# One attention program with its setup inside, batch 0 split on two engines, the top-token search spread over two turns, and the weights turned one group a unit

## What is computed

```python
x = x + _layernorm(_L0_attn_ref(_layernorm(x), ...))
x = x + _layernorm(_L0_ffn_ref(_layernorm(x), ...))   # top_k(scores, 128) per batch
x = x + _layernorm(_L1_attn_ref(_layernorm(x), ...))  # top_k(m, 35) per head
x = x + _layernorm(_L1_ffn_ref(_layernorm(x), ...))
```

## Time and profile before

| what | us |
|---|---|
| median of 3 runs | 2881.6 (2872.1 to 2886.0) |
| the profiled execution | 2883.1 |
| its span, first to last instruction | 2881.3 |
| busy in it: PE | 2537.3 (88%) |
| busy in it: DVE | 1708.3 (59%) |
| busy in it: ACT | 1199.1 (42%) |
| busy in it: POOL | 914.3 (32%) |

### The profile page before, as it was taken

The page is one execution under the profiler, slowest core; times in us unless marked ns, Lnnn a source line. Parts: engine busy times, 40 slices in busy tenths (PEclk is TensorE's granted clock), DMA queues, the critical chain, the costliest instruction groups (busy, mean ns, idle before and its releaser), DMA issues. The chain is left out here.

```text
span 2881.3 us, 40813 instructions
## 1 busy us (share of the span) xinstructions
PE 2537.3 (88%) x14324; PEld 1509.3 (52%) x14324; DVE 1708.3 (59%) x4753; ACT 1199.1 (42%) x1949; POOL 914.3 (32%) x1444
## 2 busy tenths in 40 slices
PE   3699999999999999999628999966999899999997
PEld 2244445454444445443316888844566665666664
DVE  2667676775867677678748754725444254344442
ACT  1166665666666665656313332122232222222321
POOL 6040352606143251704041211113323315224142
PEclk9699999999999999999658999978999999999999
DMA  2434061524326051531110211231112111011010
GB/s 93 132 100 109 24 193 54 182 54 147 105 72 180 24 177 53 172 98 48 45 57 9 71 53 65 82 103 60 31 37 67 30 45 60 31 59 45 16 44 30
DMA packets 156167, 220.28 MB, mean 76 GB/s; under 512 B 18639, under 2 KB 123035, under 8 KB 149724
## 3 DMA queue, kind: packets, MB, share of 16 engines
q1 hardware_dynamic: 151868, 213.65, 24.3%
q0 software_dynamic: 4096, 4.01, 0.5%
HBM read 113.75 MB, written 103.88 MB: 76 GB/s over the span
## 5 line engine op out<-in xcount | busy, mean ns | idle before, releaser
L1064 ACT ACTIVATE pt<-ps 128x1024 f32<-128x1024 f32 (+3 forms) x768 | 601.7, 812 | 306.5 <-PE ps L962 210.8
L856 DVE CUSTOM_DVE_ANT_0 masked<-ps,mask_q 128x128 bf16<-128x128 f32 (+3 forms) x1024 | 473.3, 485 | 244.9 <-PE ps L940 242.4
L940 PE MATMUL ps<-sk,sq 96*128 96x512 bf16 (+3 forms) x1536 | 427.8, 337 | 65.3 <-DMA sk<-scratch_stacks 27.5
L959 PE MATMUL ps<-sq,sk 99*128 99x512 bf16 (+3 forms) x1536 | 399.9, 329 | 13.7 <-DMA sq<-scratch_nm_parts 11.7
L860 DVE TENSOR_REDUCE mx<-ps 128x1 f32<-128x512 f32 x512 | 351.8, 687 | 90.7 <-PE ps L940 90.3
L940 PEld LDWEIGHTS ps<-sk,sq 96*128 96x128 bf16 x1536 | 132.3, 97 | 384.1 <-issue 101.3
L978 PE MATMUL ps<-pt,val 128*32 128x512 f32 (+3 forms) x3072 | 327.7, 499 | 3.3 <-ACT yt L1072 3.3
L2267 PE MATMUL ps<-w_fc,eyb 128*128 128x256 f32 x1024 | 229.7, 382 | 13.7 <-ACT eyb L2328 7.8
L959 PEld LDWEIGHTS ps<-sq,sk 99*128 99x128 bf16 x1536 | 148.2, 98 | 156.5 <-ACT pt L1064 52.5
L2255 PE MATMUL ps<-eht,w_fc 128*128 128x512 f32 x512 | 224.3, 596 | 1.5 <-ACT eht L2318 1.5
L2267 PEld LDWEIGHTS ps<-w_fc,eyb 128*128 128x128 f32 x1024 | 192.9, 191 | 47.5 <-ACT eyb L2328 16.1
(11 more groups left out here) (335 smaller groups left out, 4370.9 us busy)
## 6 DMA issues: line engine op xcount, KB each, us to landing
scratch_stacks<-space SPq DMA_DIRECT2D x32, 768.0 KB, 4.0
sq<-scratch_stacks SPq DMA_DIRECT2D x32, 768.0 KB, 8.7
sk<-scratch_stacks SPq DMA_DIRECT2D x32, 768.0 KB, 9.9
scratch_stacks<-space SPq DMA_DIRECT2D x32, 512.0 KB, 5.0
scratch_x<-xr SPq DMA_DIRECT2D x16, 1024.0 KB, 7.6
space<-in_L_attn_x SPq DMA_DIRECT2D x8, 1024.0 KB, 14.0
scratch_stacks<-space SPq DMA_DIRECT2D x32, 256.0 KB, 5.5
xr<-in_L_attn_x SPq DMA_DIRECT2D x8, 1024.0 KB, 6.3
```

The source lines that it names most:

```text
L856: nc.vector.tensor_tensor_reduce(mem["masked"][:, slot, 0:n], ps[:, RING[slot], 0:n], mem["mask_q"][:, BANK - n:BANK], 1.0, -3e38, ALU.add ...
L940: nc.tensor.matmul(ps[:, bank, 0:n], sq[0:ROWS, h, i * P:(i + 1) * P], sk[0:ROWS, h, half * BANK:half * BANK + n], start=True, stop=True)\
L959: last = nc.tensor.matmul(ps[:, bank, 0:n], sk[0:ROWS_M, h, j * P:(j + 1) * P], sq[0:ROWS_M, h, q0:q0 + n], start=True, stop=not diag)
L1064: nc.scalar.activation(pt[:, u % 3, 2 * pair:2 * pair + 2, 0:n], ps[:, bank:bank + 2, 0:n], ACT.Exp, scale=SCALE).then_inc(e["exp_done"], 1)
```

## The change

It has these parts:

- The setup is no program any more. `attention_setup` returns five functions that issue its parts inside the attention program: x of batch 0 is now SP's first load; POOL's and DVE's first instructions stand at the head of their streams; the rotation of the weights stands on DVE between x_stat and x_norm of batch 0; PE's bias products stand behind the four "xt" of batch 0. Its small tables lie in the buffer att. The memset of ones over sk comes on POOL behind batch 0's parts. The barrier and the clearing between setup and attention go; waits on `made`, `biased`, `prepared`, `masked` and `ones_in` come in their place.
- Of batch 0's eight halves of parts DVE does six and POOL the first half of k in each chunk. Stack 0 is loaded behind chunk 0, stacks 1 and 2 behind chunk 1.
- `EARLY_B` is 5, `LATE_B` 3. The scores of the first five batches are turned in unit 1 of turn 6; the 16 rounds stand in every fifth unit from unit 6 of turn 6 (the last is unit 33 of turn 7), "tok" in unit 42 of turn 7.
- The weights are staged in two steps, the first with `L1_attn_Wo` in a buffer of its own ("spare"). Their 20 groups are turned one a unit: 11 in units 20 to 30, 9 in units 33 to 41 of turn 7.
- In the attention's tail "t2" of tile i stands before "proj" of tile i - 1.
- The second program has new tables of places. By them five ranking rounds instead of two precede the first k_t on DVE, the last round and "tok" come half a batch earlier, "pick" of batch 5 is the first to wait for them, "up" comes behind "o" and "val" behind "s" on PE, and SP has load b, store_q b, load b + 1, ... where it had load b + 1 before store_q b.

The diff, cut to its core:

```diff
-EARLY_B = 6
+EARLY_B = 5
...
+    def begin_sync(sp):
+        sp.dma_start(mem["x"][:, :, :], io["x"][0].rearrange("(j p) c -> p j c", p=P)).then_inc(e["x_in"], 16)
+        with nc.allow_non_contiguous_dma(reason="a few columns of a bias"):
+            for dst, src in loads:
+                sp.dma_start(dst, src).then_inc(loaded, 16)
+
...
+    def setup_vector(v):
+        v.wait_ge(loaded, 16 * len(loads))
...
+        nc.vector.tensor_copy(w["ident16"][:, :], w["ident"][:, :])
+        nc.vector.drain()
+        nc.vector.memset(groupf[:, :], 0.0).then_inc(turned, 1)
+        v.wait_ge(cols, 1)
+        nc.vector.tensor_copy(w["bqk"][:, :], ps[:, 6, 0:2 * KC]).then_inc(biased, 1)
+        v.wait_ge(rows, 1)
+        nc.vector.tensor_tensor(w["bias_proj"][:, :], ps[:, 5, 0:C], bproj[:, :], ALU.add).then_inc(prepared, 1)
...
+        nc.vector.drain()
+        v.wait_ge(masked, 1)
...
+    def setup_tensor(pe):
+        pe.wait_ge(turned, 1)
+        for n in range(2 * KC):
+            last = nc.tensor.matmul(ps[:, 6, n:n + 1], brot[0:1, n * P:(n + 1) * P], one[:, :],
+                                    start=True, stop=True)
+        last.then_inc(cols, 1)
+        for k in range(KC):
+            last = nc.tensor.matmul(ps[:, 5, 0:C], bvrep[:, k, :], w["wproj"][:, k, :],
+                                    start=(k == 0), stop=(k == KC - 1))
+        last.then_inc(rows, 1)
...
 STAGED = (
-    (("sq", (("L0_ffn_W_qkv", 0), ("L0_ffn_W_out", 1536))), ("sk", (("L0_ffn_W1", 0), ("L1_attn_Wq", 1536)))),
+    (("sq", (("L0_ffn_W_qkv", 0), ("L0_ffn_W_out", 1536))), ("sk", (("L0_ffn_W1", 0), ("L1_attn_Wq", 1536))),
+     ("spare", (("L1_attn_Wo", 0),))),
     (("sq", (("L0_ffn_W2", 0), ("L1_attn_Wk", 1536))), ("sk", (("L0_ffn_W3", 0), ("L1_attn_Wv", 1536)))),
-    (("sq", (("L1_attn_Wo", 0),)),),
 )
...
+def parts_on_vector(step):
+
+
+    _, b, r, chunk, n = step
+    return b == 0 and (r, n) != (1, 0)
...
-            put(behind + 10 + i, ("proj", b, i))
+            if i:
+                put(behind + 9 + i, ("proj", b, i - 1))
+        put(behind + 17, ("proj", b, NT - 1))
...
-        put(now + 37 + n // 2, ("weights", B - 1, n))
-    put(now + 29, ("scores", B - 1, 0))
+        put(now + (20 + n if n < 11 else 22 + n), ("weights", B - 1, n))
+    put(now - turn + 1, ("scores", B - 1, 0))
     for n in range(ROUNDS_C):
-        put(now + 34 + n, ("top", B - 1, n))
-    put(now + 52, ("tok", B - 1))
+        put(now - turn + 6 + 5 * n, ("top", B - 1, n))
+    put(now + 42, ("tok", B - 1))
...
-    order += [("xt", 0, n, k) for n in range(NHALF) for k in range(KC)]
+    order += [("xt", 0, n, k) for n in range(NHALF) for k in range(KC)] + [("setup", 0)]
     for chunk in range(KC):
         for r in range(2):
             order += [("qk", 0, r, chunk, n) for n in range(NHALF)] + [("parts", 0, r, chunk, n) for n in range(NHALF)]
-    order += [("stack", 0, s) for s in range(SETS - 1)] + [("v", 0, 0, n) for n in range(NHALF)]
+        order += [("stack", 0, s) for s in ((0,), (1, 2))[chunk]]
+    order += [("v", 0, 0, n) for n in range(NHALF)]
     order += [("max", 0, 0, n) for n in range(len(MU))] + [("nmax", 0, 0), ("rows", 0, 0), ("nm", 0, 0)]
...
-        setup_attention(nc, io, w, ps, mem)
...
+                elif kind == "stack" and step == ("stack", 0, SETS - 2):
+                    g.wait_ge(e["parts_ready"][1], NHALF * KC)
+                    nc.gpsimd.memset(mem["sk"][ROWS:P, :, :], 1.0).then_inc(e["ones_in"], 1)
+                elif kind == "parts" and not parts_on_vector(step):
                     r, chunk, n = a
                     half = slice(n * BANK, (n + 1) * BANK)
                     until_taken(g, ("qk", b, r, chunk, n))
-                    done = nth[step]
+                    done = pool_parts[step]
...
+                if step == ("x_norm", 0, 0):
+                    setup_vector(v)
+                elif kind == "parts" and parts_on_vector(step):
+                    r, chunk, n = a
+                    half = slice(n * BANK, (n + 1) * BANK)
+                    until_taken(v, ("qk", b, r, chunk, n))
+                    if chunk:
+                        v.wait_ge(e["parts_out"][r], 16 * len(RUNS[r]))
+                    nc.vector.tensor_copy(part[:, r, 0, half], qk[:, r, half])
+                    nc.vector.drain()
+                    nc.vector.tensor_tensor(qk[:, r, half], qk[:, r, half], part[:, r, 0, half], ALU.subtract)
+                    nc.vector.drain()
+                    nc.vector.tensor_copy(part[:, r, 1, half], qk[:, r, half])
+                    nc.vector.drain()
+                    nc.vector.tensor_tensor(part[:, r, 2, half], qk[:, r, half], part[:, r, 1, half], ALU.subtract)\
+                        .then_inc(e["parts_ready"][r], 1)
                 if kind == "top":
...
+                        if b == 0 and s == 0:
+                            pe.wait_ge(e["prepared"], 1)
+                            pe.wait_ge(e["masked"], 1)
...
+                        if b == 0 and s == 0:
+                            pe.wait_ge(e["ones_in"], 1)
...
-                    if halves_before(b, *a) >= NHALF:
+                    if halves_before(b, *a) == 0:
+                        act.wait_ge(e["biased"], 1)
+                    elif NHALF <= halves_before(b, *a) < (KC + 1) * NHALF:
+                        act.wait_ge(e["parts_ready"][r], halves_before(b, r, chunk, 0))
+                    elif halves_before(b, *a) >= NHALF:
...
-    0, 151.5, 157.5, 165.5, 169, 173.5, 180, 185.5, 192, 192.5, 205, 210.5, 224.5, 230, 233, 233.5,
+    0, 96, 96.5, 105, 108, 114, 119.5, 124.5, 133.5, 139, 150.5, 151, 165, 167, 179.5, 188.5,
 )
-TOK_AT = (239, 240)
+TOK_AT = (191, 188.5)
 
```

More of the change, by code:

```diff
@@ L360, in weight_groups @@
         for buffer, names in places:
-            place = mem[buffer][:, s * HS:(s + 1) * HS, :].rearrange("p h t -> p (h t)").bitcast(F32)
+            if buffer == "spare":
+                place = mem["spare"]
+            else:
+                place = mem[buffer][:, s * HS:(s + 1) * HS, :].rearrange("p h t -> p (h t)").bitcast(F32)
             for name, at in names:
@@ L599, in attention_loop @@
             .rearrange("p (r a t) -> p r a t", r=2, a=PARTS)
-        names = """padded gains_in sc_out sc_in idx_ready
+        names = """loaded made masked zeroed turned cols rows numbered biased prepared ones_in padded gains_in sc_out sc_in idx_ready
             x_in x_stat head_step x_rstd x_ready
@@ L670, in until_split @@
                 engine.wait_ge(e["parts_out"][2 * chunk + r], 16 * len(RUNS[r]) * B)
+    begin_sync, begin_gpsimd, begin_vector, setup_vector, setup_tensor = attention_setup(nc, io, w, ps, mem, e)
+    pool_parts, halves = {}, 0
+    for step in order:
+        if step[0] == "parts":
+            pool_parts[step] = halves
+            halves += not parts_on_vector(step)
     with nc.Block() as block:
@@ L674, in _ @@
         def _(sp):
+            begin_sync(sp)
             for step in order:
@@ L751, in _ @@
         def _(g):
+            begin_gpsimd(g)
             for step in order:
@@ L826, in _ @@
         def _(v):
+            begin_vector(v)
             for step in order:
@@ L916, in _ @@
                         pe.wait_ge(taken[slot], uses)
-                if kind == "weights":
+                if kind == "setup":
+                    setup_tensor(pe)
+                elif kind == "weights":
                     s, turns, _ = groups[a[0]]
@@ L983, in _ @@
                     n, k = a
+                    if b == 0:
+                        pe.wait_ge(e["made"], 5)
                     pe.wait_ge(e["x_ready"], NT * b + 4 * (n + 1))
@@ L1138 @@
 PRODUCTS_AT = {
-    ("hnt",): (148, 143), ("q_t",): (152, 153), ("k_t",): (157.5, 153.5), ("s", 0): (159, 159.5),
[7 rows of a table removed]
+    ("hnt",): (105.5, 103.5), ("q_t",): (110, 111), ("k_t",): (112, 113), ("s", 0): (114.5, 115),
[7 rows of a table added]
 }
 OTHERS_AT = {
-    ("l1",): 133, ("xs",): 139, ("hn",): 141.5, ("pick",): 149, ("r1",): 157.5, ("less", 0): 160.5,
-    ("exp", 0): 161.5, ("exp", 1): 163, ("less", 1): 163, ("hn2",): 188, ("r2",): 205, ("load",): 207,
-    ("x2",): 208.5, ("xn2",): 211, ("r3",): 223, ("r4",): 225.5, ("put",): 230, ("samp",): 240.5,
-    ("store_q",): 240.5,
+    ("l1",): 93, ("xs",): 96, ("hn",): 98, ("pick",): 107.5, ("r1",): 111, ("exp", 0): 115.5, ("exp", 1): 117,
+    ("less", 0): 117, ("less", 1): 118, ("hn2",): 144.5, ("r2",): 155, ("x2",): 165, ("xn2",): 168.5, ("r3",): 177,
+    ("r4",): 181.5, ("put",): 189, ("samp",): 191.5, ("load",): 207.5, ("store_q",): 210.5,
 }
 RANKS_AT = (
-    0, 151.5, 157.5, 165.5, 169, 173.5, 180, 185.5, 192, 192.5, 205, 210.5, 224.5, 230, 233, 233.5,
+    0, 96, 96.5, 105, 108, 114, 119.5, 124.5, 133.5, 139, 150.5, 151, 165, 167, 179.5, 188.5,
 )
-TOK_AT = (239, 240)
+TOK_AT = (191, 188.5)
 def mod_order():
```

241 lines of the change are left out of this document (99 added, 142 removed), and 14 rows, old and new, of the table PRODUCTS_AT.

## The result

| | before | after |
|---|---|---|
| median of the runs | 2880.4 us (17 runs) | 2889.4 us (17 runs, 2885.4 to 2894.9) |
| ratio to before | | 1.0039, 95% interval 1.0028 to 1.0050 |
| span of the profiled execution | 2881.3 us | 2890.6 us |
| mean granted clock | 0.945 | 0.949 |

The changed kernel is 9 us slower, by my bound of 0.5% no change. I had forecast 2854, with 2822 to 2880: the time lies outside. The gains that I counted came, the two large ones larger than I said. Three costs took them back, of which I had one at six tenths of its size, one at a sixth and one at nothing.

A forecast was written before the change was run, and what follows sets the result against it. PE was taken to set the pace of the attention (busy 156.1 of 163.8 us in turn 6), with 48 us of slack on DVE. Sum: 2883.1 - 30 + 35 - 33 - 3 + 2 = 2854 us, range 2822 to 2880.

The forecast's parts named there:

- start: Start of the attention: first products at 59 to 60 instead of 89.1, -30 us (bounds -24 and -34).
- steady turns, swap of t2 and proj: Steady attention turns: the swap costs nothing, since exp products stand between the two steps either way.
- top rounds in turns 6 and 7: Turns 6 and 7: each of 16 DVE rounds stalls PE 2.2 us, +35 in all (bounds 0 and 64).
- weights: Weight groups moved from the last unit set into units 20 to 35: -3 us (0 to -7).
- tail: Attention's tail: 21 to 22 us at full clock where 55.0 stood, -33; -24 if the clock falls anyway.
- POOL chain: 38.7 us of POOL work after the attention's projections, expected to stay unchanged.
- second program: Second program ranks three batches instead of two, five rounds ahead of the first k_t: +2 us (bounds -2.5 and +9.5).
- rival (c): Stalls let the clock fall: rounds cost 64 + 22 = 86, total 2905; sign, turn 6 clock under 0.95. Chance 0.05.
- Rival (b): Each round stalls PE its full 4.0 us, 64 in all: 2883, no change; sign, turn 6 30 longer. Chance 0.17.
- Rival (d): Second program's late start not made up, new order worse: +12, 2866; sign, over 8 us longer. Chance 0.08.
- rival (a): Turns 6 and 7: rounds absorbed to about 0.5 us each, 2827; sign, turn 6 unchanged. Chance 0.15.
- The price that the prediction drew from it: Start: by the shared-port lock POOL's 3.7 us would be added to the chunk, making the start worth -26.

The follow-up runs named there:

- e5: Changed kernel with the sixteen top rounds back behind the last nmax, one a unit from unit 34 of turn 7, still five early batches: 2859.8 us, ratio 0.9934.
- c1: Changed kernel with six early batches, old second-program lists, old t2/proj order in batches 0 to 6, rounds only where DVE serves nobody: 2810.9 us, ratio 0.9766.
- the control: Another name for e5, the changed kernel with the sixteen top rounds back behind the last nmax: 2859.8 us, ratio 0.9934.
- e2: Changed kernel with the old order (proj of a tile ahead of t2 of the next) for batches 0 to 6: 2874.5 us, ratio 1.0008.
- e3: Changed kernel with the second program's sixteen rounds placed later, one instead of five ahead of the first k_t: 2899.3 us, ratio 1.0093.
- e7: Changed kernel with the second program's old slot lists, its rounds over slots 0 and 151.5 to 217, tokens at 220: 2886.3 us, ratio 1.0028.
- e4: Changed kernel with all halves of q and k of batch 0 split on POOL, as before the change: 2897.8 us, ratio 1.0084.

## Why the prediction was wrong

By its own steps, predicted and found:

| step | predicted | found |
|---|---|---|
| start | -30 | -32.2 at the first nmax |
| steady turns, swap of t2 and proj | 0 | +12.0 up to batch 6 |
| the same swap in turns 6 and 7 | 0 | +1.4 and +1.6 |
| top rounds in turns 6 and 7 | +35 | +59.7 |
| weights | -3 | +2.5 in turn 7, -5.8 in the last set |
| tail | -33 | -38.5 |
| POOL chain | 0 | +0.1 |
| second program | +2 | +12.4 |
| third program | 0 | -3.8 |
| sum | -29 | +9.3 (9.4 by the rounded rows) |

The rows of turns 6 and 7 come from kernels that differ there in one part: the rounds from the changed kernel less e5; the swap from e5 less before in turn 6 and from e5 less c1 in turn 7; the weights in turn 7 from c1 less before (c1 has them at their new units, but neither the swap nor a round ahead of the last nmax). Single profiles scatter by some tenths of a us there, so rows of 1 to 3 us are rough.

**The start** went as described: q,k products at 29.59 (30.0), the first cast of a half at 34.05 (34.5), sk asked for at 49.98 (50), first product at 56.85 (59 to 60). A half took DVE 2.5 us alone, as worked out from the slopes. Two sizes were off and partly cancel: beside POOL the splitting of chunk 0 ended at 43.5 instead of 42.0, and the load of sk took 6.9 us instead of 10.0.

**The rounds** are the largest miss, 25 us, and the failing step is "a stall of 2.2 us a round, 16 x 2.2 = 35", taken as the whole price. PE's idle is 35.6 us in sixteen rounds, my 35. I had the other half of the price in hand, in rival (c): that stalls let the clock fall, at 2.7 us for half the rounds, 1.35 a round. It came at 24.1, or 1.5 a round. I had it decide only in a world in which each round stalls PE by 4.0, and argued from turn 6 before the change, where waits of under 1 us leave 1.00. The 2.4 us waits are another kind. The idle part and the clock part belong in one sum; that sum, 35 + 22, would have given 2876. Rival (b) had 64 for the rounds, close to the 59.7, but by a stall of the full 4.0 each; its total would be near by luck. Of the signs I set, three came: turn 6 over 30 us longer (b), a granted clock under 0.95 there (c), the second program over 8 us longer (d). The Trainium skill, page "TensorE: Matmul & The Clock Gate", section "A second HAM failure mode: psum-queue depth-cycling", describes a clock that swings when short idles cut groups of products while the banks cycle. The trace agrees: 1.00 in the control's turn 6, 0.92 with nine rounds in it, and half rate in the products right behind a round.

**"In the steady turns the swap costs nothing: exp products stand between the two steps either way"** is the second failing step. By e2 it costs 1.9 us in each of turns 1 to 5, some 9 of the 12.0, and by the ledger 3 more in turns 6 and 7. The rest of the 12.0 is mostly one set of batch 2, 45.1 us instead of 41.7, which is 43 to 46 in all kernels with the new start: there the returned maxima are late once, 2.3 us of PE wait, and the set's clock is 0.96. Why they are late there I have not followed.

**The second program** failed at "But those 12 us are then missing from the stretch to 1625". The first kbd came 9.8 later, as worked out (9.5), but what the later stretch gave back was not kept: kbd of batch 4 was 4.8 behind before, that of batch 6 9.0, and the end 12.4. Rival (d) had +12 on the sum with a chance of 0.08; found is +10.4 on it. Its reason was not right: neither the late start (e3) nor the new order (e7) makes the loss, but the third late batch.

**The tail** ran at full clock; a tile cost PE 1.09 us instead of the 1.5 I took, and it is 16.5 where I had 21 to 22. I put the full clock down to the missing rounds; by e5 the projections have it in the new order even with the rounds back, so in the last batch the swap is worth some 14 us by itself, about what it costs in the turns before. **The weights** came out net -3.3 for -3: 2.5 paid in turn 7, 5.8 back in the last set.

The chances: 0.73 on faster leant on rival (a), absorbed rounds, for a fifth of it. Nothing was absorbed. Three terms erred the same way, rounds, swap and second program by 50 us together, and the start, the tail and the third program gave only 11.5 back; the range of 26 us upwards did not hold two misses at once.

## What to carry to other kernels

Price a long instruction on the consumer of a short ring twice: by its length less what the ring covers, and by the clock of the producer after the stall, here 2.2 + 1.5 us for a block of 4.0. Cutting it helped by half only; the place for it is where nobody waits for its engine, and such places can be found in the trace as windows in which another engine's serial chain runs: six of sixteen rounds fitted into a POOL chain for nothing. A change with several parts is worth taking apart: the start and the last batch's order of this one, with its rounds moved and without its steady order and its third late batch, took 2811 us where the kernel before took 2881.5 on the same chip.

## What was not expected of the hardware

DVE and POOL make each other wait while both split halves in SBUF. Beside POOL a cast of 512 columns on DVE took 1.05 and 1.22 us instead of 0.43, a subtraction 0.94 instead of 0.69; beside DVE, POOL's first cast took 0.89 instead of 0.61 and its subtraction 1.48 instead of 1.15. A half cost POOL 4.8 instead of 3.7 and DVE 4.1 instead of 2.5. The two streams of the changed kernel, merged in order of time:

```profile
38.66 1.48 POOL L780 TENSOR_TENSOR space<-space 128x512 f32<-128x512 f32 x1
39.38 1.05 DVE L850 CAST space<-space 128x512 bf16<-128x512 f32 x1 [0.25 <-ACT space L1142]
...
40.97 1.48 POOL L785 TENSOR_TENSOR space<-space 128x512 bf16<-128x512 f32 x1
41.51 1.22 DVE L854 CAST space<-space 128x512 bf16<-128x512 f32 x1
```

Add start and length: the casts of DVE end 0.29 and 0.28 us behind the POOL subtraction in whose course they start, whether they last 1.05 or 1.22, and the subtraction of DVE ends 0.54 behind POOL's cast. It is the same in chunk 1 (0.28; 0.54 and 0.55) and the other way round: POOL's subtractions end 1.00 to 1.01 behind DVE's, its casts 0.46 to 0.47 behind DVE's. So the one that starts second does its work when the first has ended; its recorded length holds the wait. The Trainium skill, page "SBUF — State Buffer", section "SBUF: two separate sides", has one engine wait for the other's whole instruction, and the trace agrees. The price that the prediction drew from it was too high: the whole 3.7 us of POOL's half would be added only if DVE had stood through all of it, but the two take turns, and the three halves of DVE in chunk 0 took 9.5 us (34.05 to 43.50) instead of 7.5. DVE's help was still worth 4.6 us at the first product (e4).

A single wait of 2.3 us, where the same set of the next batch has 0.5, stands in a set of batch 2 that took 3.3 longer (45.1 against 41.8); the granted clock was 0.96 over it, against 1.00 in that next one.

The third program, the same instructions in every kernel, took 1006.4 us in the profile before and 1001.0 to 1003.9 in those of all eleven others. Against the changed kernel, at the same instruction of ACT each time, 2.7 of the 3.8 us have come by 560 us into it and the rest in the last 100. This was not explained, and 3.8 us of the ledger rest on it.
